# A fused attention and mixture-of-experts block: twelve uneven turns per attention unit, and one stage joined to the next

## The chip, the cores and the metric

One core of one Trainium2 chip runs the whole program in one launch. The metric is the device time of one execution in microseconds, the median of several runs. TensorE (PE) multiplies, VectorE (DVE), ScalarE (ACT) and GpSimd (POOL) work on what it leaves in PSUM, and SyncE (SP) issues most DMAs.

## The reference

Two batches of 2048 tokens of width 256, 16 heads of width 16, everything in float32:

```
mod = silu(c) @ w_mod                       # sa, ca, ga, sb, cb, gb per batch
h = layernorm(x) * (1 + ca) + sa
q = (h @ W_q + b_q) @ W_s;  k = h @ W_k + b_k;  v = h @ W_v + b_v
attn = softmax(q k^T / sqrt(16)) v          # per head, 2048 x 2048 scores
x = x + ga * (attn @ W_o + b_o)
h = layernorm(x) * (1 + cb) + sb
scores = softmax(h @ router_w + router_b)   # 8 experts
each expert takes its 512 best tokens:  relu(h1 @ w1 + b1) @ w2 + b2, times the score
x = x + gb * (sum of the experts' rows)
```

## The kernel before

The program is a row of stages, each a block in which the five engines run their own instruction lists and meet only at semaphores. All engines meet at the end of a block.

**Projection and attention** are one block already. Attention has 32 heads (2 batches of 16), each cut into two halves of 1024 queries: 64 units. A unit has three kinds of work for TensorE:

- 16 *groups* (`fill_group`, L216 to L221): two matmuls, 48 contraction rows each, 512 columns, the first on partitions 0 to 47, the second on partitions 64 to 111. They give unscaled scores with queries on partitions, only to find each query's maximum. VectorE takes the maximum of a group of 128x1024 in one instruction (`reduce_group`, L227). There are two slots of two PSUM banks, so group n may start when the reduce of group n-2 is done (`groups_out`, L904). Groups run 24 ahead of the scores.
- 32 *score chunks* (`scores`, L553 to L570): one matmul of 50 contraction rows and 512 columns. Even chunks lie on partitions 0 to 49, odd ones on 64 to 113. ScalarE takes exp of each chunk (L869) from one of three PSUM banks, so chunk n may start when the exp of chunk n-3 is done (`scores_out`).
- the *value products* (`weigh`, L908 to L926), 128 contraction rows, accumulated in bank 7. They are done in blocks: `BLOCK` = 3 chunks at a time, the first block of a unit 2 chunks, so 11 blocks and 11 turns per unit. Four column strips of 32 go side by side, in two instructions each. A block's products are issued `DELAY` = 2 turns after its scores.

One turn of TensorE (loop at L932 on) is: the value products of an old block, then three new score chunks with one or two groups among them. In five turns of a unit, which start on an even chunk, two groups stand around the scores (G0 G1 S0 S1 S0 G0 G1); in five, which start on an odd chunk, one group stands after the first score (S1 G0 G1 S0 S1); one turn has one group and two chunks (G0 G1 S0 S1). After its last product of a unit ScalarE copies the accumulator out (`take_output`, L855), between the exps of chunk 2 and 3 of the next unit.

**The post stage** is the next block (L979 to L1146). For 8 chunks of 512 tokens: output projection (`project`, L1114), residual (DVE L1047), layernorm statistics (L1053, L1058, L1061; ScalarE's square root L1022; five Newton steps L165 to L169), normalised rows (L1067), eight transposes (`turn_h2`, L1098), scale and shift (ScalarE L1010), routing logits (`route`, L1123), eight transposes back (`turn_rows`, L1132), a copy (L1017) and a store of the rows to DRAM. TensorE's order for chunk n is `turn_h2(n-2)`, `project(n)`, `route(n-2)`, `turn_rows(n-2)`; VectorE does residual, root and normalisation of chunk n in one body. The first two 2 MB pairs of expert weights are loaded at this block's start (L982, L983).

**The selection stage** is the block after it: the softmax of the logits and a search of 30 probes for each expert's threshold, in which VectorE and TensorE alternate (L1270 and L1341). Then come the expert stage's gathers and matmuls, which the change does not touch.

Of the kernel before, what the change touches and what calls it, by code (L numbers as in the profile page):

```python
# [10 lines left out]
ALU = mybir.AluOpType  # L11
# [80 lines left out]
def adaln_moe_block(nc, x, w_q, b_q, w_k, b_k, w_v, b_v, w_o, b_o, w_s, router_w, router_b,  # L92
                    w1, b1, w2, b2, c, w_mod, out):
    ctx = ExitStack()
    with ctx:
# [596 lines left out]
        xb_in, xb_ready = [sem(f"xb_in{b}") for b in range(NB)], sem("xb_ready")  # L692
        with nc.Block() as block:
            pv_done, acc_out, v_staged = sem("pv_done"), sem("acc_out"), sem("v_staged")
# [5 lines left out]
            normalised = sem("normalised")  # L700
# [3 lines left out]
            def blocks_until(n):  # L704
                u, c = divmod(n, UNIT_CHUNKS)
                return u * BLOCKS + (c - FIRST_BLOCK) // BLOCK + 2

            def chunks_of(block):
                u, b = divmod(block, BLOCKS)
                end = u * UNIT_CHUNKS + FIRST_BLOCK + b * BLOCK  # L710
                return range(end - (BLOCK if b else FIRST_BLOCK), end)
# [21 lines left out]
            def _(sp):  # L733
# [38 lines left out]
                for u in range(UNITS):  # L772
# [15 lines left out]
                    if u % HALVES and u // HALVES + NBUF < G:  # L788
                        load_next(u // HALVES)
                finish_group(UNITS - 2)  # L790
                store_output(UNITS - 1)
                load_output(UNITS - 1)

            @block.gpsimd
            def _(pool):
# [38 lines left out]
                for u in range(1, UNITS):  # L834
# [10 lines left out]
                    if u > 2 and done % HG == HG - 1:  # L845
                        normalise_part(done // HG, f)

            @block.scalar
            def _(act):
# [7 lines left out]
                for n in range(STEPS * 2):  # L857
                    if n % UNIT_CHUNKS == BLOCK and n > UNIT_CHUNKS:
                        take_output(n // UNIT_CHUNKS - 1)
# [11 lines left out]
                take_output(UNITS - 1)  # L871

            @block.vector
            def _(dve):
# [13 lines left out]
                invert(UNITS - 2)  # L888

            @block.tensor  # L890
            def _(pe):
# [41 lines left out]
                for block in range(DELAY, blocks):  # L933
                    weigh(block - DELAY)
                    b = block % BLOCKS
                    many = FIRST_BLOCK if b == DELAY else BLOCK
                    twice = b != DELAY and (b == 0 or b > DELAY and b % 2 == 1) or block == 2 * DELAY
                    for n in range(many):
                        if n == (0 if twice or b == DELAY else 1) and group < STEPS:
                            next_group(group)  # L940
                            group += 1
                        scores(pe, *divmod(chunk, 2))
                        chunk += 1
                    if twice and group < STEPS:
# [6 lines left out]
        h2_t = pt[:, 1:4:2, :].rearrange("p s (k t) -> p s k t", k=KD)  # L951
        ao_c = stage_a[:].rearrange("p s (t d) -> p s t d", d=D)
        xn2 = stage_b[:].rearrange("p s (t d) -> p s t d", d=D)
        h2_c = pt[:, 0:4:2, :].rearrange("p s (t d) -> p s t d", d=D)
        w_slots = v_all[:].rearrange("p t d -> p (t d)").rearrange("p (s n) -> p s n", s=2)
        w1_sb = [w_slots[:, s, 0:KD * FF].rearrange("p (k f) -> p k f", k=KD) for s in range(2)]
        w2_sb = [w_slots[:, s, KD * FF:].rearrange("p (f d) -> p f d", f=NF) for s in range(2)]
        w1_v = w1.rearrange("e (k p) f -> e p k f", p=P)
        w2_v = w2.rearrange("e (f p) d -> e p f d", p=P)
        w1_h = [kp[:, s, :].rearrange("p (k f) -> p k f", k=KD) for s in range(2)]  # L960
        weights_in = [sem(f"weights_in{s}") for s in range(2)]
        w1_high, w1_low = sem("w1_high"), sem("w1_low")

        def take_w1_high(act, e):
            act.wait_ge(weights_in[e % 2], e // 2 * 32 + 32)
            nc.scalar.copy(w1_h[e % 2], w1_sb[e % 2]).then_inc(w1_high, 1)

        out_stored = sem("out_stored")
        h2_stored = [sem(f"h2_stored{p}") for p in range(2)]
        h2_ready, xn2_ready, rows_turned = (sem(n) for n in ("h2_ready", "xn2_ready", "rows_turned"))  # L970
        y_full, y_out = sem("y_full"), sem("y_out")
        h2_turned, h2t_ready, l_full, l_out = sem("h2_turned"), sem("h2t_ready"), sem("l_full"), sem("l_out")
        var2_done, root2_done = sem("var2_done"), sem("root2_done")
        b_of = lambda n: slice(n // NCH, n // NCH + 1)

        with nc.Block() as block:
            @block.sync
            def _(sp):
                for par in range(2):  # L979
                    sp.sem_inc(h2_stored[par], 16)  # L980
                for e in range(2):
                    sp.dma_start(w1_sb[e], w1_v[e]).then_inc(weights_in[e], 16)  # L982
                    sp.dma_start(w2_sb[e], w2_v[e]).then_inc(weights_in[e], 16)  # L983
                for n in range(chunks):
                    if n == 2:
                        sp.wait_ge(normalised, G // HG * HALVES - 2)
                        load_inverse(sp, G // HG - 1, 1)
                    rows = slice(n * CT, (n + 1) * CT)
                    sp.wait_ge(y_out, n * 2 + 4)
                    sp.dma_start(out_rows[:, rows, :], xb[:, rows, :]).then_inc(out_stored, 16)  # L990
                    sp.wait_ge(h2_ready, n * 2 + 2)
                    sp.dma_start(h2_rows[:, rows, :], h2_c[:, n % 2]).then_inc(h2_stored[n % 2], 16)
                sp.wait_ge(out_stored, 16 * chunks)
                for par in range(2):
                    sp.wait_ge(h2_stored[par], 16 * pairs + 16)

            @block.gpsimd
            def _(pool):
                for f in range(HALVES):
                    pool.wait_ge(o_in[f], G * 32)  # L1000
                    pool.wait_ge(inverse_in[f], G * 16)
                    normalise(nc.gpsimd, G // HG - 1, f).then_inc(normalised, 1)

            @block.scalar
            def _(act):
                def take_h2(n, par):
                    act.wait_ge(h2_turned, n + 3)
                    act.wait_ge(l_full, n + 1)
                    for k in range(KD):
                        nc.scalar.activation(h2_t[:, par, k, :], bank(4 + k), ACT.Identity,  # L1010
                                             bias=mod_col[:, 2, k, b_of(n)], scale=mod_col[:, 3, k, b_of(n)]).then_inc(h2t_ready, 1)

                def take_rows(n, par):
                    act.wait_ge(rows_turned, n + 1)
                    act.wait_ge(h2_stored[par], n // 2 * 16 + 16)
                    for half in range(2):
                        nc.scalar.copy(h2_c[:, par, 2 * half:2 * half + 2, :],  # L1017
                                       bank(half).rearrange("p (t d) -> p t d", d=D)).then_inc(h2_ready, 1)

                def root(n, par):  # L1020
                    act.wait_ge(var2_done, n + 1)
                    nc.scalar.activation(nwt[:, 1, par * CT:(par + 1) * CT], nwt[:, 0, par * CT:(par + 1) * CT],  # L1022
                                         ACT.Sqrt).then_inc(root2_done, 1)

                act.sem_inc(h2t_ready, 2)
                for n in range(chunks):
                    if n > 1:
                        take_h2(n - 2, n % 2)
                    root(n, n % 2)
                    if n > 1:  # L1030
                        take_rows(n - 2, n % 2)
                for n in range(chunks - 2, chunks):
                    take_h2(n, n % 2)
                    take_rows(n, n % 2)

            @block.vector
            def _(dve):
                link, v = links["dve"], nc.vector
                dve.sem_inc(l_out, 2)
                dve.sem_inc(y_out, 2)  # L1040

                def body(n, par, logits_of):
                    for half in range(2):

                        dve.wait_ge(y_full, n * 2 + (half + 5))
                        rows = xb[:, bass.ds(n * CT + half * 2, 2), :]
                        v.tensor_tensor(rows, bank(2 + half).rearrange("p (t d) -> p t d", d=D), rows,  # L1047
                                        ALU.add).then_inc(y_out, 1)
# [583 lines left out]
```

## Time and profile before

| | us |
|---|---|
| median of 3 runs (lowest, highest) | 1806.25 (1805.63, 1806.42) |
| the profiled execution | 1805.18 |
| its span, first to last instruction | 1803.2 |
| attention, from the first value product to the last | 143 to 1406 |
| post stage | 1412 to 1486 |
| selection stage | 1486 to about 1570 |

The span is some 2 us under its execution's time, and that execution is 1.1 us under the median. The stage borders are read from the timeline. In a timeline the start of a matmul can be trusted more than its end, which is modelled, so durations of a turn are taken from start to start.

### The profile page before, as it was taken

To read this page: it belongs to the slowest core of one execution; us is meant where nothing else is said; L and a number is where in the kernel's file an instruction comes from. 1 tells how busy PE (TensorE), PEld (TensorE's weight loads), DVE (VectorE), ACT (ScalarE), POOL (GpSimd) and SP (SyncE) were. 2 spreads that over 40 slices of the span, in tenths; PEclk is the share of its full clock that TensorE was granted. 3 is DMA by queue.
4 is the path that set the end of the run, shared out by engine and by line. 5 is a ranking of instruction groups with operands and counts; after the bars stand their busy time and mean duration, and the time that the engine had idled before them with its cause. 6 is when DMAs were issued, how large, how long until landed. Compare 5 with 4: busy or idle time off the path is not lost. (4 is left out here: it accounts for less than half of the span.)

```text
span 1803.2 us, 42958 instructions
## 1 busy us (share of the span) xinstructions
PE 1692.5 (94%) x16862; PEld 951.5 (53%) x16862; DVE 1495.3 (83%) x1964; ACT 1215.3 (67%) x2304; POOL 245.8 (14%) x306
## 2 busy tenths in 40 slices
PE   7999999999999999999999999999999771599997
PEld 4645555555555555555555555555554670267886
DVE  5579999999999999999999999999995458645652
ACT  2327888888888888888888888888888330022231
POOL 0332013000000000000000000000000001235553
PEclk9999999999999999999999999999999885599999
DMA  7560442222233222223322222332200440025342
GB/s 253 189 180 28 101 97 39 38 41 38 52 64 52 38 40 40 38 52 63 51 41 39 41 37 52 61 53 41 39 14 14 145 164 0 24 74 137 83 128 24
DMA packets 93652, 121.95 MB, mean 68 GB/s; under 512 B 24060, under 2 KB 70716, under 8 KB 90348
## 3 DMA queue, kind: packets, MB, share of 16 engines
q1 hardware_dynamic: 84492, 109.22, 26.9%
q0 software_dynamic: 6144, 8.39, 2.7%
q8 instruction: 133, 2.18, 0.5%
q10 hardware_dynamic: 2816, 1.61, 0.3%
q14 instruction: 67, 0.55, 0.1%
HBM read 79.35 MB, written 38.54 MB: 65 GB/s over the span
## 5 line engine op out<-in xcount | busy, mean ns | idle before, releaser
L227 DVE TENSOR_REDUCE pmax<-ps 128x2 f32<-128x1024 f32 x1024 | 1192.6, 1216 | 53.2 <-PE ps L220 46.3
L869 ACT ACTIVATE pt<-ps 128x512 f32<-128x512 f32 x2048 | 1077.7, 599 | 181.4 <-PE ps L569 170.3
L220 PE MATMUL ps<-kp,qp 48*128 48x512 f32 x2048 | 626.5, 464 | 2.4 <-DVE pmax L227 2.4
L923 PE MATMUL ps<-pt,v_st 128*32 128x256 f32 (+1 forms) x10752 | 589.7, 335 | 0.2 <-ACT pt L869 0.2
L569 PE MATMUL ps<-qp,kp 50*128 50x512 f32 x2048 | 562.5, 422 | 0.5 <-ACT pt L869 0.5
L569 PEld LDWEIGHTS ps<-qp,kp 50*128 50x128 f32 x2048 | 294.4, 185 | 258.7 <-ACT pt L869 250.9
L923 PEld LDWEIGHTS ps<-pt,v_st 128*32 128x32 f32 x10752 | 265.7, 109 | 265.3 <-issue 192.3
L220 PEld LDWEIGHTS ps<-kp,qp 48*128 48x128 f32 x2048 | 246.1, 184 | 115.0 <-issue 90.0
L1452 ACT ACTIVATE ao<-ps,b_col 128x512 f32<-128x512 f32 x64 | 44.0, 688 | 156.5 <-PE ps L1591 156.5
L210 POOL CAST m_parts<-rowmax_t 128x32 fp32r<-128x32 f32 x64 | 13.4, 210 | 839.7 <-DVE rowmax_t L239 839.7
L1605 PE MATMUL ps<-v_all,ao 128*128 128x256 f32 x512 | 112.5, 381 | 0.8 <-ACT ao L1452 0.8
L1605 PEld LDWEIGHTS ps<-v_all,ao 128*128 128x128 f32 x512 | 96.7, 190 | 14.1 <-ACT ao L1452 1.2
L431 ACT ACTIVATE pt<-ps,xb 128x512 fp32r<-128x512 f32 x32 | 22.0, 687 | 61.3 <-PE ps L594 61.3
L1527 DVE TENSOR_TENSOR pt<-ps,b_row 128x256 f32<-128x256 f32 x32 | 13.5, 422 | 57.9 <-PE ps L1605 57.9
L594 PE MATMUL ps<-pt,xb 128*128 128x512 f32 x128 | 59.1, 603 | 1.7 <-ACT pt L415 1.7
L1420 POOL DMA_INDIRECT y<-pt,scatter_at x32 | 54.8, 1711 | 33.3 <-DVE pt L1531 24.9
L798 POOL COPY v_st<-v_all 128x256 f32<-128x256 f32 x32 | 12.6, 397 | 293.3 <-PE ps L923 293.3
L1490 DVE TENSOR_TENSOR stage_b<-lane,col_row 128x1024 bf16<-128x1024 int32 x32 | 37.7, 1222 | 13.4 <-PE ps L1564 13.1
L1444 ACT COPY list_t<-ps 128x128 f32<-128x128 f32 x8 | 2.1, 259 | 67.0 <-PE ps L1564 67.0
L1402 POOL DMA_INDIRECT stage_a<-h_rows,gather_at x32 | 33.0, 1032 | 84.5 <-DVE gather_at L1501 54.3
L1591 PE MATMUL ps<-qp,kp 128*128 128x512 f32 x96 | 40.0, 416 | 0.0
L1114 PE MATMUL ps<-wog,ao 128*128 128x256 f32 x128 | 33.3, 422 | 6.8 <-DVEq L1040 6.8
(196 smaller groups left out, 944.0 us busy)
## 6 DMA issues: line engine op xcount, KB each, us to landing
kp<-k_parts SPq DMA_DIRECT2D x186, 128.0 KB, 4.5
v_all<-L_ffn_w SPq DMA_DIRECT2D x16, 1024.0 KB, 8.4
qp<-q_parts SPq DMA_DIRECT2D x186, 64.0 KB, 4.0
q_parts<-pt SPq DMA_DIRECT2D x16, 512.0 KB, 2.7
k_parts<-pt SPq DMA_DIRECT2D x16, 512.0 KB, 3.0
o_rows<-o_sb SPq DMA_DIRECT2D x64, 128.0 KB, 2.0
sums_c<-o_rows SPq DMA_DIRECT2D x512, 0.5 KB
m_rows<-m_parts SPq DMA_DIRECT2D x256, 2.0 KB
```

What stands on the lines that cost most here:

```text
L220: last = nc.tensor.matmul(slot[:, half * CH:(half + 1) * CH], qp[rows, r, a * P:(a + 1) * P], kp[rows, r, c * CH:(c + 1) * CH], start=True ...
L227: v.reduce_max(pmax[:, u % 2, 2 * k:2 * k + 2], slot.rearrange("p (f t) -> p f t", f=2), AX.X).then_inc(groups_out, 1)
L569: nc.tensor.matmul(bank(n % SCORE_BANKS), kp[rows, h % NBUF, kt * P:(kt + 1) * P], qp[rows, h % NBUF, f * CH:(f + 1) * CH], start=True, st ...
L594: last = mm(unit_bank(n, u), w[:, k, (u % 2) * P:(u % 2 + 1) * P], h_t[n % 2][:, k, :], start=k == 0, stop=k == KD - 1)
L869: nc.scalar.activation(pt[:, s % PTS, half * CH:(half + 1) * CH], bank(n % SCORE_BANKS), ACT.Exp, scale=SCALE).then_inc(scores_out, 1)
L923: last = mm(acc[32 * j:32 * (j + 1), first * QB:(first + many) * QB], v_st[:, h % NBUF, kt, :], probs[:, :, j * QB:(j + 1) * QB], start=kt ...
L1114: last = mm(bank(2 + half)[:, t * D:(t + 1) * D], ao[:, n // NCH * KD + k, at:at + P], wog[:, n // NCH, k, :], start=k == 0, stop=k == KD - 1)
L1420: nc.gpsimd.indirect_dma_start(out_flat, bass.IndirectOffsetOnAxis(ap=scatter_at[:, par, cc:cc + 1], axis=0), contrib[:, cc, :], None, com ...
L1452: nc.scalar.activation(hid[:, f, :], bank(2 + f % 2), ACT.Relu, bias=b1_col[:, bass.ds(e * NF + f, 1)]).then_inc(hid_out, 1)
L1490: v.tensor_tensor(one_hot[:, g8 % 2], lane[:, bass.ds(n, 1), g8 * 8:(g8 + 1) * 8].squeeze(1).unsqueeze(2).broadcast_to([P, 8, P]), col_row ...
L1591: last = mm(bank(2 + f % 2), w[:, k, f * P:(f + 1) * P], t[:, k, :], start=i == 0, stop=i == len(products) - 1)
L1605: last = mm(bank(eo_banks[cc])[:, 0:D], hid[:, f, cc * P:(cc + 1) * P], w2_sb[par][:, f, :], start=f == 0, stop=f == NF - 1)
```

## The change

1. `BLOCK`, `FIRST_BLOCK` and the rule for one or two groups go. A table of twelve turns replaces them. Each entry is (chunks weighed, chunks scored, places of the groups among the scores):

```diff
-BLOCK = 3
-BLOCKS = -(-UNIT_CHUNKS // BLOCK)
-FIRST_BLOCK = UNIT_CHUNKS - (BLOCKS - 1) * BLOCK
+TURNS = ((3, 3, (1, 2)), (3, 3, (1,)), (3, 3, (1, 3)), (2, 3, (2,)), (2, 2, (1,)), (2, 2, (1,)),
+         (1, 2, (0,)), (2, 2, (1,)), (3, 3, (2, 3)), (3, 3, (2,)), (4, 3, (0, 3)), (4, 3, (1,)))
+BLOCKS = len(TURNS)
+BLOCK_ENDS = [sum(TURNS[(i + DELAY) % BLOCKS][0] for i in range(b + 1)) for b in range(BLOCKS)]
```

```diff
                 for block in range(DELAY, blocks):
                     weigh(block - DELAY)
-                    many = FIRST_BLOCK if b == DELAY else BLOCK
-                    twice = b != DELAY and (b == 0 or b > DELAY and b % 2 == 1) or block == 2 * DELAY
+                    _, many, groups_before = TURNS[block % BLOCKS]
+                    for n in range(many + 1):
+                        if n in groups_before and group < STEPS:
+                            next_group(group)
+                            group += 1
+                        if n < many:
+                            scores(pe, *divmod(chunk, 2))
+                            chunk += 1
...
+                    if block == blocks - DELAY:
+                        project_rows(pe, 0)
                 for block in range(blocks - DELAY, blocks):
                     weigh(block)
-
+                post_pe(pe)
```

2. The post stage moves into the attention block. Its instruction lists follow each engine's attention list, and chunk 0's output projection is issued before attention's last turn and last two value blocks. The orders of its engines change:

```diff
+        def post_dve(dve, link, invert_first, invert_last):
...
+            residual(0)
+            invert_first()
+            for n in range(chunks):
+                if n + 1 == 3:
+                    invert_last()
+                if n + 1 < chunks:
+                    residual(n + 1)
+                normalise_rows(n)
+                if n > 0:
+                    take_logits(n - 1)
...
+        def post_pe(pe):
...
+            project_rows(pe, 1)
+            for n in range(chunks):
+                turn_h2(n)
+                if n + 2 < chunks:
+                    project_rows(pe, n + 2)
+                route(n)
```

`residual(n)` waits for both halves of `project_rows(n)` and ends with the variance; `normalise_rows(n)` is the Newton steps and the normalised rows; `turn_h2(n)` waits for those. ScalarE takes the last unit's accumulator out after chunk 0's square root. SyncE, before attention's last unit, issues the loads of the first two experts' weights.

3. The transposes back, their copies and the row stores leave the post stage. TensorE now does them in the selection stage, half a chunk (four transposes) after every second of the 30 probe matmuls; ScalarE copies and SyncE stores there. TensorE's probe loop is unrolled:

```diff
+                    for j in range(TOPBIT + 1):
                         pe.wait_ge(counted, j + 1)
                         mm(bank(1)[:, 0:1], same[:], count[:], start=True, stop=True).then_inc(totalled, 1)
+                        if j % 2 and j // 2 + 2 < 2 * chunks:
+                            turn_rows(j // 2 + 2)
```

## Rows read from the trace of the kernel before

**Rows 1.** The page: instructions and busy share of each engine.

```profile
PE 1692.5 (94%) x16862; PEld 951.5 (53%) x16862; DVE 1495.3 (83%) x1964; ACT 1215.3 (67%) x2304; POOL 245.8 (14%) x306
```

**Rows 2.** Busy time by stage: length, engines, granted clock, DMA share, GB/s.

```profile
150.00:1375.00 1225.00, 1224.80 (x14378) 621.87 (x14379) 1175.80 (x1123) 1054.54 (x2045) 72.58 (x163) 1.00 0.27 47
1375.00:1405.00 30.00, 29.81 (x336) 14.62 (x332) 2.79 (x5) 26.47 (x53) 0.46 (x2) 1.00 0.11 30
1412.40:1486.40 74.00, 63.74 (x384) 57.78 (x384) 44.98 (x169) 21.38 (x41) 4.38 (x2) 0.87 0.51 178
1486.40:1570.00 83.60, 20.93 (x133) 10.24 (x133) 62.24 (x263) 3.00 (x6) 19.71 (x32) 0.51 0.05 13
```

**Rows 3.** Groups by line, busy, mean ns, idle before; one timeline row of VectorE.

```profile
L227 DVE TENSOR_REDUCE pmax<-ps 128x2 f32<-128x1024 f32 x1024 | 1192.6, 1216 | 53.2 <-PE ps L220 46.3
L869 ACT ACTIVATE pt<-ps 128x512 f32<-128x512 f32 x2048 | 1077.7, 599 | 181.4 <-PE ps L569 170.3
...
803.99 5.71 DVE L227 TENSOR_REDUCE pmax<-ps 128x2 f32<-128x1024 f32 x5
```

**Rows 4.** The line that copies the accumulator out, once per unit: first and last.

```profile
L855 ACT COPY o_sb<-ps x64: 372/393/395, 163.1 to 1405.7; 128x256 f32<-128x256 f32 x64
```

**Rows 5.** Timeline of TensorE in attention: start, length, line, operands, count.

```profile
801.83 0.50 PE L220 MATMUL ps<-kp,qp 48*128 48x512 f32 x2
...
802.98 0.86 PE L923 MATMUL ps<-pt,v_st 128*32 128x128 f32 x16
...
807.58 0.49 PE L569 MATMUL ps<-qp,kp 50*128 50x512 f32 x1
...
808.48 0.86 PE L923 MATMUL ps<-pt,v_st 128*32 128x256 f32 x16
...
815.87 0.64 PE L923 MATMUL ps<-pt,v_st 128*32 128x256 f32 x8
816.44 0.50 PE L220 MATMUL ps<-kp,qp 48*128 48x512 f32 x2
816.78 0.40 PE L569 MATMUL ps<-qp,kp 50*128 50x512 f32 x2
817.11 0.86 PE L923 MATMUL ps<-pt,v_st 128*32 128x256 f32 x16
817.89 0.50 PE L220 MATMUL ps<-kp,qp 48*128 48x512 f32 x2
```

**Rows 6.** Timeline of TensorE: the end of a turn with two groups.

```profile
809.84 0.46 PE L220 MATMUL ps<-kp,qp 48*128 48x512 f32 x1
809.85 0.45 PE L569 MATMUL ps<-qp,kp 50*128 50x512 f32 x1
...
810.13 0.39 PE L220 MATMUL ps<-kp,qp 48*128 48x512 f32 x1
```

**Rows 7.** Timeline between attention's last value block and the selection stage's first instruction.

```profile
1404.78 0.86 PE L923 MATMUL ps<-pt,v_st 128*32 128x128 f32 x16 [0.19 <-ACT pt L869]
...
1412.48 10.19 PE L1114 MATMUL ps<-wog,ao 128*128 128x256 f32 x32 [6.84 <-DVEq L1040]
...
1486.47 0.25 DVE L1251 TENSOR_SCALAR same_i<-iota_i 128x128 int32<-128x128 int32 x1 [6.00 <-PEq L976]
```

**Rows 8.** Timeline of one chunk of the post stage, VectorE and TensorE.

```profile
1451.92 0.69 DVE L1047 TENSOR_TENSOR xb<-ps,xb 128x512 f32<-128x512 f32 x1 [0.72 <-PE ps L1114]
...
1454.33 1.04 PE L1098 MATMUL ps<-ident,stage_b 128*128 128x128 f32 x8
...
1455.15 0.18 DVE L165 RECIPROCAL rstd<-nwt 128x4 f32<-128x4 f32 x1 [0.27 <-ACT nwt L1022]
1455.20 3.62 PE L1114 MATMUL ps<-wog,ao 128*128 128x256 f32 x16
...
1456.15 1.39 DVE L1067 TENSOR_SCALAR stage_b<-xb,mv,rstd 128x256 f32<-128x256 f32 x4
```

**Rows 9.** Timeline of TensorE at the post stage's end, after it had stood idle.

```profile
1471.36 1.95 PE L1123 MATMUL ps<-rw_sb,pt 128*128 128x8 f32 x16 [2.11 <-ACT pt L1010]
...
1474.83 1.91 PE L1098 MATMUL ps<-ident,stage_b 128*128 128x128 f32 x8
```

More of the change, by code:

```diff
@@ new lines, in y_bank, with turned_bank, logits_bank, post_sp @@
+        def y_bank(half):
+            return bank(3 + half)
+        def turned_bank(k):
+            return bank(5 + k)
+        def logits_bank(n):
+            return bank(2 + 5 * (n % 2))
+        b_of = lambda n: slice(n // NCH, n // NCH + 1)
+        def post_sp(sp, load_last_inverse):
+            for n in range(chunks):
+                if n == 2:
+                    load_last_inverse()
+                rows = slice(n * CT, (n + 1) * CT)
+                sp.wait_ge(y_out, n * 2 + 2)
+                sp.dma_start(out_rows[:, rows, :], xb[:, rows, :]).then_inc(out_stored, 16)
+            sp.wait_ge(out_stored, 16 * chunks)
@@ new lines, in project_rows @@
+        def project_rows(pe, n):
+            if n == 0:
+                pe.wait_ge(xb_ready, 2 * NB)
+                pe.wait_ge(groups_out, STEPS)
+                pe.wait_ge(normalised, G // HG // NB * HALVES)
+            if n >= NCH and n % 2 == 0:
+                pe.wait_ge(normalised, (G // HG - 1) * HALVES + (n - NCH) // 2 + 1)
+            for half in range(2):
+                if n > 0:
+                    pe.wait_ge(y_out, n * 2 + half - 1)
+                for t in range(2):
+                    at = (n % NCH) * CH + (half * 2 + t) * P
+                    for k in range(KD):
+                        last = nc.tensor.matmul(y_bank(half)[:, t * D:(t + 1) * D], ao[:, n // NCH * KD + k, at:at + P],
+                                                wog[:, n // NCH, k, :], start=k == 0, stop=k == KD - 1)
+                last.then_inc(y_full, 1)
@@ new lines, in post_pe, with turn_h2, route @@
+        def post_pe(pe):
+            def turn_h2(n):
+                pe.wait_ge(xn2_ready, n + 1)
+                if n > 0:
+                    pe.wait_ge(h2t_ready, n * 2)
+                for k in range(KD):
+                    for t in range(CT):
+                        last = nc.tensor.transpose(turned_bank(k)[:, t * P:(t + 1) * P], xn2[:, n % 2, t, k * P:(k + 1) * P], ident[:])
+                last.then_inc(h2_turned, 1)
+            def route(n):
+                pe.wait_ge(h2t_ready, n * 2 + 2)
+                if n == 1:
+                    pe.wait_ge(acc_out, UNITS)
+                if n > 1:
+                    pe.wait_ge(l_out, n - 1)
+                for t in range(CT):
+                    for k in range(KD):
+                        last = nc.tensor.matmul(logits_bank(n)[:, t * E:(t + 1) * E], h2_of(n)[:, k, t * P:(t + 1) * P],
+                                                rw_sb[:, k, :], start=k == 0, stop=k == KD - 1)
+                last.then_inc(l_full, 1)
+            project_rows(pe, 1)
+            for n in range(chunks):
+                turn_h2(n)
+                if n + 2 < chunks:
+                    project_rows(pe, n + 2)
+                route(n)
@@ L846, in _ @@
                         normalise_part(done // HG, f)
+                for f in range(HALVES):
+                    normalise_part(G // HG - 1, f)
             @block.scalar
@@ L940, in _ @@
                             next_group(group)
                             group += 1
-                        scores(pe, *divmod(chunk, 2))
-                        chunk += 1
-                    if twice and group < STEPS:
+                        if n < many:
+                            scores(pe, *divmod(chunk, 2))
+                            chunk += 1
+                    if block == 2 * DELAY:
                         next_group(group)
                         group += 1
+                    if block == blocks - DELAY:
+                        project_rows(pe, 0)
@@ L1206, in adaln_moe_block, with _ @@
             with nc.Block() as block:
+                @block.sync
+                def _(sp):
+                    for n in range(chunks):
+                        sp.wait_ge(h2_ready, n * 2 + 2)
+                        sp.dma_start(h2_rows[:, n * CT:(n + 1) * CT, :], h2_c[:, n % 2]).then_inc(h2_stored[n % 2], 16)
+                    for par in range(2):
+                        sp.wait_ge(h2_stored[par], 16 * pairs)
                 @block.gpsimd
@@ L1245, in _ @@
                     nc.scalar.activation(logits[:], logits[:], ACT.Exp).then_inc(exps_done, 1)
+                    for g in range(2 * chunks):
+                        n, half = divmod(g, 2)
+                        act.wait_ge(rows_turned, g + 1)
+                        if n > 1 and half == 0:
+                            act.wait_ge(h2_stored[n % 2], n // 2 * 16)
+                        nc.scalar.copy(h2_c[:, n % 2, half * 2:half * 2 + 2, :],
+                                       bank(6 + half).rearrange("p (t d) -> p t d", d=D)).then_inc(h2_ready, 1)
                 @block.vector
```

294 lines of the change are left out of this document (107 added, 187 removed).

## The prediction

> **What bounds the kernel now.** I read the page first [rows 1]. TensorE is busy 94% of the span and VectorE 83%. A busy TensorE in this profile may be waiting inside an instruction, so I then read the busy times by stage [rows 2]. The stretch from 150 to 1375 us holds two thirds of the time; in it TensorE is booked full at the full clock, VectorE 96%, ScalarE 86%. Which of the three sets the pace?
>
> The accumulator is copied out once per unit, so the first and last copy give the unit's length: (1405.7 - 163.1) / 63 = 19.72 us [rows 4]. VectorE needs for its 16 reduces one start every (5.71 - 1.22) / 4 = 1.12 us when it never waits [rows 3], 17.9 us a unit, and some 0.5 us for the two small steps at a unit's end: 18.5. ScalarE's exps were busy 1077.7 / 64 = 16.8 us a unit [rows 3]. So both have over a microsecond to spare, and VectorE's idle time before its reduces, 53.2 us in all [rows 3], is time in which TensorE was late. TensorE is the bound, and what counts is what one turn of it costs.
>
> The timeline gives that, start to start [rows 5]. A turn has a value part and a score part.
>
> - Value part: 2 chunks take 816.44 - 815.87 = 0.57 us, 3 chunks 817.89 - 817.11 = 0.78. So 0.21 a chunk and 0.15 per turn.
> - Score part: the two matmuls of a group stand in one row of 0.50 us, x2, as long as one alone (0.49, x1); so do an even and an odd score (0.40, x2). They lie on different halves of the partitions and run side by side. I call such a pair, or one matmul left alone, a *slot*. G0G1 | S0S1 is 2 slots: 817.11 - 816.44 = 0.67 us. S1G0 | G1S0 | S1 is 3 slots: 808.48 - 807.58 = 0.90. G0G1 | S0S1 | S0 | G0G1 is 4: 802.98 - 801.83 = 1.15. Some 0.23 to 0.25 per slot and 0.2 per turn.
>
> Only neighbours in the program pair. [Rows 6] show it: the group's first matmul is booked beside a score on the same partitions, at 809.84, and its partner starts only at 810.13, 0.29 us later. It did not slip ahead beside the lone score.
>
> Counted so, the present unit needs: value parts 11 x 0.15 + 32 x 0.21 = 8.37; score parts 5 x 1.15 + 5 x 0.90 + 0.67 = 10.92; together 19.29. The other 0.43 us of the 19.72 are waits, for exps (three banks) and reduces (two slots).
>
> **The change, part 1: twelve turns.** What can be won is the 0.43 us of waits. What is added comes out of the table. One more turn: 0.15 us in the value part and the 0.2 fixed in the score part. And the order of scores and groups changes which matmuls are neighbours. From turn 2, with the parity of the chunk:
>
> - turns 2, 8, 10, 0 have two groups and come to 4 slots each (turn 2: S0 | G0G1 | S1S0 | G0G1; turn 0: S0 | G0G1 | S1G0 | G1S0)
> - turns 3, 9, 11, 1 have one group and 3 scores or 3 slots each (S1S0 | G0G1 | S1 or S1G0 | G1S0 | S1)
> - turns 4, 5, 7 have one group between two scores: S0 | G0G1 | S1. Four matmuls in 3 slots, where G0G1 | S0S1 would have been 2
> - turn 6 is G0G1 | S0S1, 2 slots
>
> So 4 x 1.15 + 7 x 0.90 + 0.67 = 11.57, value parts 12 x 0.15 + 6.72 = 8.52, together 20.09 us, against 19.72 measured now. I followed the events through one unit with the starts above (a reduce every 1.12 us, an exp every 0.53, which is 1077.7 / 2048 in [rows 3]): with twelve smaller turns hardly a wait is left, so I take 20.09 as it stands. That is +0.37 us a unit. Some 61 units run with all three kinds of work: +22.6 us. From both sides: if the waits stay at half, +0.58 a unit, +35 us. On the other side five turns (0, 2, 4, 5, 7) now begin with a lone score right behind the value products. No row shows that. In the present kernel the first slot behind them takes 816.78 - 816.44 = 0.34 instead of 0.23; if a lone first score hides in that, 5 x 0.11 = 0.55 us come off, and the unit is 19.54 plus waits: -11 us or less. I take the upper figure, since the pair there takes 0.50 us for both, no longer than one alone [rows 5], so the extra time is not the second one's.
>
> A rule speaks further against the new order. The Trainium skill, "TensorE: Matmul & The Clock Gate", section "Part 3: Packing small matmuls", says matmuls start and end strictly in program order and that a weight load overlaps running matmuls only when its row group differs. By it each lone score that is followed by a group on its own rows would also pay for the load; [rows 6] show 0.06 of that (0.29 for 0.23), and three such places (turns 4, 5, 7) are not in my 0.90. It would make 0.2 us a unit more, +11 us, by an estimate from these rows.
>
> The end of attention, 1.6 units without groups (second row of [rows 2]), waits for exps and changes little: 0, within 1 us.
>
> **Part 2: the joined post stage.** Won: the gap from the last value block, 1404.78 + 0.86, to the first projection at 1412.48, 6.8 us [rows 7], and transposes back (8 of about 0.12 us) from a TensorE-bound stage. Chunk 0's projection, 3.6 us [rows 8], now lies before the last turn; behind it the exps catch up, which hides about 0.8, so attention ends 2.8 us later, at 1408.4 on the old clock. Projection 1 follows at once and ends at 1412.1.
>
> What is late next is the new order. VectorE does `residual(n+1)` before `normalise_rows(n)`, and TensorE does `project_rows(n+2)` after `turn_h2(n)`, which waits for `normalise_rows(n)`. So VectorE, done with chunk n's rows, waits for a projection that starts only now; nothing overlaps but `route`. One lap, from rows ready to rows ready: 0.06 wake-up; transposes 1455.20 - 1454.33 = 0.87; projection 3.62 + 0.04; from the second half's residual to normalised rows 1456.15 - 1451.92 = 4.23 less 0.27 waited for the root = 3.96; rows 1.39 [rows 8]. Sum 9.9 us, at the full clock. The present loop overlaps all this and takes about 7 us a chunk (8 in the 74 us of [rows 2], third row). In a lap TensorE works 0.87 + 3.6 + 1.9 (the routing, 1.95 in [rows 9]) and then stands about 3.5 us. After standing 2.11 us in the present kernel its eight transposes took 1.91 instead of 1.04 [rows 8, 9], and after 6.84 us the 32 projection matmuls took 10.19, so 5.1 per chunk instead of 3.62 [rows 7]: the clock is then at its lower level, 1.2 GHz (0.87 granted over the stage, [rows 2]). With 1.9 and 5.1 the lap is 12.3 us. Part of each lap will run at 2.4 GHz; I take 11.5. The Trainium skill's same page, section "HAM oscillation", describes such a loop, cold again after every gap; it would give the 12.3.
>
> Rows of chunk 0 are ready at 1412.1 + 3.96 + 1.39 = 1417.5; six laps, 69 us; then the last two chunks' transposes, scale and routing, about 11 us (one chunk with rows back and store took 1486.47 - 1474.83 = 11.6 [rows 7, 9]; two without these take about as long). The selection stage starts at 1497.5 instead of 1486.5: +11 us, between 0 (9.9 a lap) and +17 (12.3).
>
> The last unit's accumulator, stores, inverses and the POOL product have until the third lap (chunk 4) and the fifth (chunk 6): 1437 and 1457; they need some 12 and 30 us from 1409, so they are hidden, and would cost a few us if not. SyncE's four weight loads wait behind a staging that is long done, and DMA is 11 to 27% busy there [rows 2]: 0.
>
> **Part 3: transposes in the selection.** TensorE is busy 20.9 of 83.6 us there (fourth row of [rows 2]). Four cold transposes take 0.95 us (half of 1.91, [rows 9]) between two probe matmuls. VectorE needs about 1 us to come with its next count, so they are just hidden: +1, between 0 and +13 (14 times 0.95).
>
> **The sum.** Span 1803.2 + 22.6 + 11 + 1 = 1837.8; the profiled execution lay 2.0 above its span, and the median 1.1 above that: 1841. I say 1840.
>
> **Rivals.**
> 1. *The lone first score hides behind the switch from value products*, and waits of about 0.1 are left: 19.64 us a unit, -5 us; with the post stage +11 and +1: 1813. Against it, the 0.50 us of the first pair. 0.15.
> 2. *The unit gains, and the whole is faster.* The array lets S0, G0, G1, S1 finish in two slots (the odd half running ahead), and the lone score hides. Turns 4, 5, 7 cost 0.67: 3 x 0.23 + 0.55 = 1.24 off 20.09, 18.85, so VectorE's 18.5 and waits set it: about 19.2, 0.5 less than now, -31 us; with +12 behind it 1787. It decides from a unit of 19.5. Against it [rows 6]; for it, that nothing shows the matmul behind such a pair. With only half of that gain 1797 to 1803. 0.22 in all.
> 3. *The clock stays at 2.4 GHz in the post stage*: laps of 9.9, 1840 - 11 = 1829. 0.15, since 2.11 us of standing was enough once.
> 4. *The twelve turns do nothing* (waits come back as fast as turns shrink): +0, post +12: 1818. 0.08.
> My forecast, 1840, has 0.40; its own range is 1827 to 1853.
>
> A measurement here can tell 0.2%, 3.6 us, from no change. Faster: rival 2, 0.22. Within: the lucky edge of rivals 1 and 2, 0.08. Slower: the rest, 0.70. The range, to hold it 8 times in 10, goes from 1798, inside rival 2, to 1851.
>
> **What the profile after would show.** The accumulator copies 20.1 us apart (19.5 or less would refute the slots). VectorE's idle before its reduces risen, from 53 to about 75 us, and ScalarE's too. A turn S0 G0 G1 S1 of 0.90 from first start to next value block, not 0.67. In the post stage normalised rows 10 to 12 us apart, VectorE waiting for the projection about 4 us in each, clock rows between 0.5 and 1. Half-chunk transposes between probes, with the probes' spacing unchanged. Rows of the post stage 7 us apart would make part 2 wrong.

## The result, and the profile after

The changed kernel takes 1830.2 us in the median of 4 runs (1829.2 to 1831.1), against 1806.3 for the kernel before on the same chip: a ratio of 1.0136, 95% interval 1.0120 to 1.0152. It is slower. I had forecast 1840, with 1798 to 1851 as the range.

First the rows of the new page that answer to [rows 1] and [rows 3]. Then the stages that answer to [rows 2], with the columns as there: attention, the post stage, the selection stage.

```profile
PE 1712.4 (94%) x17374; PEld 994.0 (54%) x17374; DVE 1495.9 (82%) x1964; ACT 1221.5 (67%) x2304; POOL 245.6 (13%) x306
...
L229 DVE TENSOR_REDUCE pmax<-ps 128x2 f32<-128x1024 f32 x1024 | 1188.5, 1216 | 62.9 <-PE ps L222 55.0
L1046 ACT ACTIVATE pt<-ps 128x512 f32<-128x512 f32 x2048 | 1076.4, 598 | 186.7 <-PE ps L571 166.6
```

```profile
150.00:1375.00 1225.00, 1220.30 (x14794) 648.65 (x14796) 1166.26 (x1118) 1052.86 (x2035) 72.47 (x163) 1.00 0.27 47
...
1414.00:1512.70 98.70, 65.16 (x304) 58.11 (x305) 45.87 (x158) 13.87 (x27) 4.72 (x3) 0.74 0.17 56
1512.70:1596.00 83.30, 36.62 (x199) 21.10 (x200) 62.75 (x264) 12.74 (x22) 19.59 (x32) 0.51 0.19 64
```

Busy totals hardly tell the two kernels apart. The stages do. The post stage, from the last value block to the first selection instruction, now takes 98.7 us; before it took 1486.47 - 1405.64 = 80.8 [rows 7], although a gap of 6.8 us was taken out of it. Its granted clock is 0.74, where it was 0.87 behind that gap [rows 2].

The unit is read from the accumulator's copies, as in [rows 4]:

```profile
L1032 ACT COPY o_sb<-ps x64: 353/374/394, 162.1 to 1414.5; 128x256 f32<-128x256 f32 x64
```

(1414.5 - 162.1) / 63 = 19.88 us instead of 19.72. The last of these 63 intervals has chunk 0's projection in it; the mean of the 61 before the last two is 19.86, against 19.77.

The 25.5 us between the two spans are: attention ends 8.4 us later; the post stage is 17.9 longer; selection and experts are 0.8 shorter. Attention's start moves by more than a microsecond between the runs of this case (141.9 to 145.0 us), and I did not look for the reason. From the first copy of the accumulator to the end of the last value block, which leaves the start out, the changed kernel takes 1251.9 us and the kernel before 1242.6.

One lap of the new post stage, VectorE and TensorE, answers to [rows 8]:

```profile
1460.36 1.38 DVE L789 TENSOR_SCALAR stage_b<-xb,mv,rstd 128x256 f32<-128x256 f32 x4
...
1461.79 1.97 PE L837 MATMUL ps<-ident,stage_b 128*128 128x128 f32 x8 [3.45 <-DVE stage_b L789]
1463.56 5.66 PE L826 MATMUL ps<-wog,ao 128*128 128x256 f32 x16
...
1467.21 0.69 DVE L770 TENSOR_TENSOR xb<-ps,xb 128x512 f32<-128x512 f32 x1 [5.38 <-PE ps L826]
1469.05 1.85 PE L848 MATMUL ps<-rw_sb,ao 128*128 128x8 f32 x16
1469.25 0.69 DVE L770 TENSOR_TENSOR xb<-ps,xb 128x512 f32<-128x512 f32 x1 [1.34 <-PE ps L826]
...
1472.91 1.38 DVE L789 TENSOR_SCALAR stage_b<-xb,mv,rstd 128x256 f32<-128x256 f32 x4
```

Two waits feed each other here. TensorE stands 3.45 us for VectorE's rows; then its transposes (1.97 us, at the lower clock; 1.04 at the full one [rows 8]) and its projection come one after another while VectorE stands 5.38 us. From rows to rows it is 12.55 us.

### The profile page after: what moved, and what is told of

Same layout as the page of the kernel before. It is cut to its first block and busy times, and to the rows that moved or that the text cites. A ratio compares the mean times of both kernels' runs of the same rounds, so it can differ in the third digit from the quotient of the medians.

```text
span 1828.7 us, 43907 instructions
## 1 busy us (share of the span) xinstructions
PE 1712.4 (94%) x17374; PEld 994.0 (54%) x17374; DVE 1495.9 (82%) x1964; ACT 1221.5 (67%) x2304; POOL 245.6 (13%) x306
## 5 line engine op out<-in xcount | busy, mean ns | idle before, releaser
L229 DVE TENSOR_REDUCE pmax<-ps 128x2 f32<-128x1024 f32 x1024 | 1188.5, 1216 | 62.9 <-PE ps L222 55.0
L571 PE MATMUL ps<-qp,kp 50*128 50x512 f32 x2048 | 644.3, 439 | 0.5 <-ACT pt L1046 0.5
L1105 PE MATMUL ps<-pt,v_st 128*32 128x128 f32 (+1 forms) x11264 | 603.3, 328 | 0.7 <-ACT pt L1046 0.7
L222 PE MATMUL ps<-kp,qp 48*128 48x512 f32 x2048 | 581.8, 443 | 7.3 <-DVE pmax L229 2.5
L1105 PEld LDWEIGHTS ps<-pt,v_st 128*32 128x32 f32 x11264 | 274.1, 109 | 301.3 <-issue 134.0
L571 PEld LDWEIGHTS ps<-qp,kp 50*128 50x128 f32 x2048 | 303.3, 185 | 215.8 <-ACT pt L1046 145.4
L222 PEld LDWEIGHTS ps<-kp,qp 48*128 48x128 f32 x2048 | 241.7, 184 | 98.5 <-DVE pmax L229 50.4
L212 POOL CAST m_parts<-rowmax_t 128x32 fp32r<-128x32 f32 x64 | 13.4, 210 | 838.0 <-DVE rowmax_t L241 838.0
L770 DVE TENSOR_TENSOR xb<-ps,xb 128x512 f32<-128x512 f32 x16 | 11.1, 692 | 66.8 <-PE ps L826 66.8
L1541 DVE TENSOR_TENSOR pt<-ps,b_row 128x256 f32<-128x256 f32 x32 | 13.5, 422 | 58.2 <-PE ps L1619 58.2
L837 PE MATMUL ps<-ident,stage_b 128*128 128x128 f32 x64 | 15.6, 424 | 29.9 <-DVE stage_b L789 29.9
```

What stands on the lines that cost most here:

```text
L222: last = nc.tensor.matmul(slot[:, half * CH:(half + 1) * CH], qp[rows, r, a * P:(a + 1) * P], kp[rows, r, c * CH:(c + 1) * CH], start=True ...
L229: v.reduce_max(pmax[:, u % 2, 2 * k:2 * k + 2], slot.rearrange("p (f t) -> p f t", f=2), AX.X).then_inc(groups_out, 1)
L571: nc.tensor.matmul(bank(n % SCORE_BANKS), kp[rows, h % NBUF, kt * P:(kt + 1) * P], qp[rows, h % NBUF, f * CH:(f + 1) * CH], start=True, st ...
L1105: last = mm(acc[32 * j:32 * (j + 1), first * QB:(first + many) * QB], v_st[:, h % NBUF, kt, :], probs[:, :, j * QB:(j + 1) * QB], start=kt ...
```

## The experiments

Each kernel was run beside the kernel before on the same chip. Where a unit is given for a kernel with the joined stage, it is (last copy - first copy) / 63, which holds 0.04 to 0.05 us of chunk 0's projection; compare it with 19.88.

**The twelve turns alone.** The kernel before with part 1 of the change (the diff of part 1 without its `project_rows` line).

> The kernel before with the table of twelve turns and nothing else of the change. Theory A (the turns cost little: in the changed kernel the accumulator copies lay 19.88 us apart against 19.72): 62 units at +0.1 to +0.16 us, so 1806.3 + 8 = 1814, unit 19.86, post stage as before. Rival B (my count of slots, 20.09 us a unit): +22.6, 1829. Rival C (the turns are free or better and all of the loss is the joined stage): 1806 or less.

Measured: 1811.7 us, ratio 1.0035 (1.0021 to 1.0049).

```profile
L856 ACT COPY o_sb<-ps x64: 366/375/393, 163.2 to 1411.4; 128x256 f32<-128x256 f32 x64
```

(1411.4 - 163.2) / 63 = 19.81 us, 0.09 above the kernel before. So the table costs 6.7 us, and my 0.37 us a unit was four times too much.

**The joined stage alone.** The changed kernel with the old turns written as a table.

```diff
-TURNS = ((3, 3, (1, 2)), (3, 3, (1,)), (3, 3, (1, 3)), (2, 3, (2,)), (2, 2, (1,)), (2, 2, (1,)),
-         (1, 2, (0,)), (2, 2, (1,)), (3, 3, (2, 3)), (3, 3, (2,)), (4, 3, (0, 3)), (4, 3, (1,)))
+TURNS = ((3, 3, (0, 3)), (3, 3, (1,)), (2, 2, (0,)), (3, 3, (0, 3)), (3, 3, (1,)), (3, 3, (0, 3)),
+         (3, 3, (1,)), (3, 3, (0, 3)), (3, 3, (1,)), (3, 3, (0, 3)), (3, 3, (1,)))
```

> The changed kernel with the eleven turns of the kernel before put back (as a table: one or two groups and 3, 3, 2, 3 ... chunks as they stood). Theory A (the two parts add up): the twelve turns alone cost 6 to 7 us, so the joined stage alone gives 1805 + 25 - 6.5 = 1823.5, the unit falls from 19.86 to 19.76 us, the post stage keeps its laps of 12. Rival B (the parts interact, the twelve turns are needed by the joined tail or hurt it): more than 3 us away from that.

Measured: 1825.0 us, ratio 1.0104 (1.0088 to 1.0121). 1.0104 x 1.0035 is 1.0139, the whole change's 1.0136: the parts add up. The joined stage is three quarters of the loss. Its attention, from the first copy to the end of the last value block, takes 1246.1 us against 1242.6 before, with units as long as before (19.77 us in the mean of the same 61). So chunk 0's projection costs 3.5 us there.

**How the array pairs matmuls.** In the changed kernel turns 4, 5 and 7 are S0 G0 G1 S1. Here is one, the third line the next value block:

```profile
802.44 0.49 PE L571 MATMUL ps<-qp,kp 50*128 50x512 f32 x1
802.45 0.72 PE L222 MATMUL ps<-kp,qp 48*128 48x512 f32 x2
...
803.11 0.65 PE L1105 MATMUL ps<-pt,v_st 128*32 128x128 f32 x16
```

803.11 - 802.44 = 0.67 us, the time of two slots, where I had counted three. It is the median of all 183 such turns.

The timeline merges the group's two matmuls into one row, but the trace behind it holds them apart, since only the second one, G1, raises the semaphore that VectorE waits for. There S0 starts at 802.444, G1 at 802.451, G0 at 802.777 and S1 at 802.789: G1, on the upper half, starts beside S0, a third of a microsecond ahead of G0, which stands before it in the program. G1 starts ahead of G0 in all 183.

The test adds matmuls on one half of the partitions only. `low_again` is 2 in turns 4, 5 and 7:

```diff
-            for half in range(2):
+            for half in [0] * low_again + [0, 1]:
                 rows = slice(HALF * half, HALF * half + KROWS)
                 last = nc.tensor.matmul(slot[:, half * CH:(half + 1) * CH], qp[rows, r, a * P:(a + 1) * P],
...
```

> The changed kernel; in turns 4, 5 and 7 (two chunks) the group's first matmul, on the lower half of the partitions, is issued three times, which writes the same values again. The order there is S0 G0 G0 G0 G1 S1. The score part of these turns takes 0.67 us in the changed kernel. Theory A (each half of the partitions is a lane of its own; a lane runs its matmuls one after another and does not wait for the order of the other): lower lane 4, upper lane 2, so 4 slots, 1.13 us. Rival B (any two run side by side): 6 / 2 = 3 slots, 0.90. Rival C (only neighbours on different halves pair, as I predicted): S0, G0, G0, G0G1, S1, 5 slots, 1.36. By A the unit grows by about 3 x 0.45 less the wait of turn 8, so by 1.0 to 1.3 us, and the time by 60 to 80.

Measured, one run: 1895.1 us, unit 20.9. One such turn, and the start of the next:

```profile
816.30 0.50 PE L571 MATMUL ps<-qp,kp 50*128 50x512 f32 x1
816.32 0.72 PE L222 MATMUL ps<-kp,qp 48*128 48x512 f32 x2
816.65 0.40 PE L571 MATMUL ps<-qp,kp 50*128 50x512 f32 x1
816.88 0.62 PE L222 MATMUL ps<-kp,qp 48*128 48x512 f32 x2
817.43 0.64 PE L1105 MATMUL ps<-pt,v_st 128*32 128x128 f32 x16
818.00 0.50 PE L571 MATMUL ps<-qp,kp 50*128 50x512 f32 x1
```

817.43 - 816.30 = 1.13 us: four slots, and 1.13 is the median of these turns too. There are six matmuls, four of them on the lower half. If any two could pair it would be 0.90, if only neighbours, 1.36. The single records show the same: on the upper half G1 starts at 816.32 and S1 at 816.65; on the lower half S0 at 816.30 and the three of the group at 816.64, 816.88 and 817.11. So each half of the partitions is a lane with its own order, and a turn's score part lasts as long as its fuller lane.

**The order that I thought cheaper.** The group ahead of both scores in those turns.

```diff
-(2, 2, (1,)), (2, 2, (1,)), (1, 2, (0,)), (2, 2, (1,))
+(2, 2, (0,)), (2, 2, (0,)), (1, 2, (0,)), (2, 2, (0,))
```

> The changed kernel with the group ahead of both scores in turns 4, 5 and 7: G0 G1 S0 S1 instead of S0 G0 G1 S1. My prediction counted 2 slots for this order and 3 for the present one. Rival C of the lane run (only neighbours pair): 3 x 0.23 us a unit less, 19.2 us, 1829 - 43 = 1786. Theory A (two lanes, each of two matmuls in either order): the turns stay at 0.67 us, the unit at 19.86 within 0.05, 1826 to 1833.

Measured: 1829.4 us, ratio 1.0135 (1.0118 to 1.0151). Nothing moved. The turn G0 G1 S0 S1 takes 0.67 us here, as S0 G0 G1 S1 did: there are two matmuls per lane in either order.

**The wait that is left.** By lanes the new table has 4 turns of four slots, 4 of three and 4 of two: 4 x 1.15 + 4 x 0.90 + 4 x 0.67 = 10.88, with the value parts' 8.52 a unit of 19.40. Measured 19.86, so 0.46 us of waits. Most of it is in turn 8:

```profile
806.08 5.71 DVE L229 TENSOR_REDUCE pmax<-ps 128x2 f32<-128x1024 f32 x5
...
806.62 0.86 PE L1105 MATMUL ps<-pt,v_st 128*32 128x256 f32 x16
807.40 0.50 PE L571 MATMUL ps<-qp,kp 50*128 50x512 f32 x2
807.74 0.39 PE L222 MATMUL ps<-kp,qp 48*128 48x512 f32 x2
807.97 0.39 PE L571 MATMUL ps<-qp,kp 50*128 50x512 f32 x1
808.44 0.50 PE L222 MATMUL ps<-kp,qp 48*128 48x512 f32 x2
808.87 0.86 PE L1105 MATMUL ps<-pt,v_st 128*32 128x128 f32 x16
```

From the score at 807.97 to the group at 808.44 it is 0.47 us instead of 0.23. The first row says why. The second of its five reduces runs from 807.18 to 808.39 in the trace, and it is the one that frees the group's PSUM slot. The group behind this standstill takes 0.43 us to the next value block. The score part is 808.87 - 807.40 = 1.47, not 1.15. The test moves one group a turn later:

```diff
-(3, 3, (2, 3)), (3, 3, (2,)), (4, 3, (0, 3)), (4, 3, (1,))
+(3, 3, (2,)), (3, 3, (0, 3)), (4, 3, (0, 3)), (4, 3, (1,))
```

> The changed kernel with one group moved from turn 8 to turn 9: turn 8 (3, 3, (2,)), turn 9 (3, 3, (0, 3)). In turn 8 the last group stands 0.47 us in the lane before it starts, the largest wait of the unit: it waits for the reduce of the group two before it. Theory A (that wait is lost time of the lane): turn 8 falls from 2.26 to about 1.67 us, turn 9 rises from 1.69 to 1.92 to 1.95, so the unit is 0.2 to 0.35 us shorter, 19.5 to 19.65: 12 to 21 us off 1829, 1808 to 1817. Rival B (VectorE or the exps are the bound and the wait only moves to another turn): unit 19.8 or more, 1825 to 1830.

Measured: 1816.7 us, ratio 1.0058 (1.0042 to 1.0075), 13.5 us less than the whole change.

```profile
L1032 ACT COPY o_sb<-ps x64: 353/376/394, 162.7 to 1401.8; 128x256 f32<-128x256 f32 x64
```

(1401.8 - 162.7) / 63 = 19.67 us instead of 19.88. The wait was real, and no other engine took its place. In the mean of the 61 intervals a unit now takes 19.65 us, less than the 19.77 of the old eleven turns.

**Is it the clock?** Six matmuls that nobody reads, after the routing of chunks 0 to 5, keep TensorE at work in the lap's gap.

```diff
                 route(n)
+                if n + 2 < chunks:
+                    for _ in range(6):
+                        nc.tensor.matmul(bank(0)[:, 0:D], ident[:], wog[:, 0, 0, :], start=True, stop=True)
```

> The changed kernel with six matmuls of 128x256 that nobody reads, after each routing of the post stage, into a bank that is free: 2.5 us of work at the full clock where TensorE now stands 3.5 us a lap. Theory A (laps of 12 us are 9.9 us of serial work plus the lower clock): the clock stays at 2.4 GHz, laps of 10.0 to 10.5, six laps give back 9 to 12 us: 1820. Rival B (the clock does not matter to the lap): laps of 12 or more and 1830 to 1836.

Measured: 1818.9 us, ratio 1.0075 (1.0060 to 1.0091), 11 us less than the change, although there is more work in it.

```profile
1460.30 1.09 PE L837 MATMUL ps<-ident,stage_b 128*128 128x128 f32 x8 [0.76 <-DVE stage_b L789]
1461.23 3.62 PE L826 MATMUL ps<-wog,ao 128*128 128x256 f32 x16
1464.68 1.85 PE L848 MATMUL ps<-rw_sb,ao 128*128 128x8 f32 x16
1466.39 2.84 PE L860 MATMUL ps<-wog,ident 128*128 128x256 f32 x12
1469.98 1.09 PE L837 MATMUL ps<-ident,stage_b 128*128 128x128 f32 x8 [0.76 <-DVE stage_b L789]
```

The lap is 1469.98 - 1460.30 = 9.68 us at the full clock. Four of the six laps were 9.7 us. The other two, 11.4 and 13.4, ran partly at the lower clock (0.84 and 0.85 granted), and in the longer one VectorE stood for a product of POOL (it multiplies the attention output by the inverses of the sums; the last section tells of it). In the changed kernel the six laps took 12.2 us in the mean, and 12.0 without the one that has such a product in it. So a lap there is 9.7 us of serial work and about 2.3 of clock.

**Which swap opens the loop.** Two kernels, each the changed one with two lines of a list exchanged. First TensorE's:

```diff
             for n in range(chunks):
-                turn_h2(n)
                 if n + 2 < chunks:
                     project_rows(pe, n + 2)
+                turn_h2(n)
                 route(n)
```

> The changed kernel with one swap in TensorE's post list: project_rows(n + 2) before turn_h2(n). Theory A (the serial lap of rows, transposes, projection, residual is what costs): residual(n+2) no longer waits for the transposes; TensorE's lap becomes projection 3.3, transposes 0.9, a wait of 1.6 for ScalarE, routing 1.9, together 7.7 us at the full clock instead of 12 us now; six laps and the tail give back about 27 us: 1803. Rival B (the laps are long because of something else, the clock alone or ScalarE): laps stay above 11 us and the time within 6 us of 1830.

Measured: 1811.5 us, ratio 1.0039 (1.0024 to 1.0054), 18.7 us less than the change where I had expected 27. The six laps were 5.5, 14.0, 7.5, 7.9, 9.6 and 9.6 us. In the one of 14.0 the routing and the projection ran at the lower clock and VectorE stood for a product of POOL.

```profile
1457.33 1.95 PE L848 MATMUL ps<-rw_sb,ao 128*128 128x8 f32 x16 [1.54 <-ACT ao L746]
...
1459.13 5.39 PE L826 MATMUL ps<-wog,ao 128*128 128x256 f32 x16
```

Routing now follows right behind the transposes and waits for ScalarE's scale and shift; the next projection stands behind it. The wait was exchanged for another one, of 1.54 us in every lap, and in some laps the clock fell behind it (5.39 us for this projection, 3.62 at the full clock).

Then VectorE's:

```diff
             for n in range(chunks):
                 if n + 1 == 3:
                     invert_last()
+                normalise_rows(n)
                 if n + 1 < chunks:
                     residual(n + 1)
-                normalise_rows(n)
```

> The changed kernel with one swap in VectorE's post list: normalise_rows(n) before residual(n + 1). TensorE's list stays. Theory A (the serial lap): VectorE then has a projection done ahead, and TensorE works transposes 0.9, projection 3.3, routing 1.9 without a wait, so laps of 6.1 to 6.9 us at the full clock; seven laps of 6.6 instead of 75.7 us in all, and the first rows some 5 us earlier: 32 to 38 us less, 1791 to 1797, under the kernel before. Rival B (the swap of the lists is not it; projection stays behind the wait, as with TensorE's swap, which left laps of 7.5 to 9.6): laps of 8 or more, 1805 or more.

Measured: 1791.2 us, ratio 0.9919 (0.9903 to 0.9936): 39 us less than the change, and faster than the kernel before.

```profile
1446.22 1.07 PE L837 MATMUL ps<-ident,stage_b 128*128 128x128 f32 x8
1447.13 3.62 PE L826 MATMUL ps<-wog,ao 128*128 128x256 f32 x16
1450.59 1.85 PE L848 MATMUL ps<-rw_sb,ao 128*128 128x8 f32 x16
1452.29 1.07 PE L837 MATMUL ps<-ident,stage_b 128*128 128x128 f32 x8
```

TensorE goes from transposes to projection to routing without standing, 6.07 us a lap here. VectorE's rows come 5.92 to 6.06 us apart, but for two laps of 7.7 and 7.9 with POOL's products in them. The post stage takes 58.1 us (1414.8 to 1472.9) instead of 98.7.

**Both parts mended.** The same swap with the old turns, and with the new table after its group was moved.

> Eleven turns as before, the joined stage, and VectorE's normalise_rows(n) before residual(n + 1). If both parts' costs are what the runs before say and add up, 1794 less 6.5 for the turns: 1785 to 1791, 0.8 to 1.1% under the kernel before. If the twelve turns help the tail: above 1791.

Measured: 1784.5 us, ratio 0.9881 (0.9865 to 0.9898). With VectorE's lines in this order the joined stage alone saves 20.5 us, where it cost 20.0.

> Twelve turns with one group moved from turn 8 to turn 9, and VectorE's rows before the next residual. If both gains add up (12.5 us for the group, 38 us for the order of lists): 1791 less 12.5, 1776 to 1782, under the eleven turns with the same order (1784.5), so that the twelve turns pay once their one long wait is gone. If the unit's gain is lost again beside the faster tail: 1784 or more.

Measured: 1777.5 us, ratio 0.9848 (0.9832 to 0.9865), beside a kernel before of 1804.2 us. It is the fastest version here. The twelve turns with the moved group beat the old eleven by 0.0033 of the time, about 6 us. The two intervals just touch, and the two kernels ran on different chips; the unit, 19.64 us against 19.77 in the two traces, says the same and gives about 8 us.

## Why the prediction was right, and where its terms were off

The direction held, and both parts of the change cost time, as forecast. The size was 10 us too large, and that it was not further off is luck. I gave 22.6 us to the twelve turns and 12 to the joined stage; alone they cost 6.7 and 20.0. The two errors half cancelled.

1. *A unit is bound by TensorE's turns, and the table adds to them.* Right in kind, wrong in size: 0.37 us a unit forecast, 0.09 measured with the turns alone. Two terms of that sum failed. The slot count: "turns 4, 5, 7 ... four matmuls in 3 slots" at 0.90 each; they took 0.67, which is 0.69 us a unit too much. I had read it out of [rows 6], and read them wrongly. I took the record at 809.84 for the group's first matmul. In the trace it is the one that raises the group's semaphore, so it is the second, on the upper half, and it starts beside the lone score on the lower half; the record at 810.13 is the first. So the group's second matmul did slip ahead, as it does in 253 of the 304 full turns with two groups of the kernel before. The length of such a turn could not have told me, since its lower lane has four matmuls and gives four slots under both readings; the single records could. And the waits: "hardly a wait is left", where 0.46 us were left. My hand count had turn 8's second group just in time; the reduce that it needed was still running. The old unit had 0.43 by the same sum. So by lanes the change takes one slot away, adds one turn, and leaves the waits as large as they were.
2. *The lone first score.* There was nothing to hide or to add. A turn that starts with a lone score and one that starts with a pair both take 0.67 us when each lane has two matmuls.
3. *The rule on the weight loads.* The Trainium skill, "TensorE: Matmul & The Clock Gate", section "Part 3: Packing small matmuls", says that a weight load overlaps only matmuls of another row group, by which these turns would cost 0.2 us a unit more. It is not borne out: 0.67 us is the time of G0 G1 S0 S1 too, both in the same kernel and in the run with the group first. Nor does that section's strict program order of starts fit: G1 starts 0.33 us ahead of G0 in the turns above.
4. *Rival 2* had the right mechanism, the odd half running ahead, and the wrong end. It took 0.55 us more off for the lone score and left 0.35 for waits, which made 19.2. Nothing came off for the lone score, and the waits were 0.46.
5. *Chunk 0's projection* inside attention: 2.8 us forecast, 3.5 measured.
6. *The serial lap*: 9.9 at the full clock forecast, 9.7 measured with the filler. This step was right, and the swap of VectorE's two lines shows it: 39 us. With the clock I took 11.5; the six laps took 73.3 us, 12.2 each, 4.3 us more. Of these 4.3 a product of POOL made about 1.9, and the clock the rest. The Trainium skill, "TensorE: Matmul & The Clock Gate", section "HAM oscillation", describes a loop that is cold again after every gap; the transposes behind the gap took 1.87 to 1.97 us in every lap, which agrees. The 12.3 us that I had worked out for such a lap was the better guess. Two bounds were also summed too wide: laps of 9.9 and 12.3 us put the post stage's part at 1.4 and 15.8 us, where I wrote 0 and 17.
7. *Before and after the laps*: from attention's end to chunk 0's rows 9.1 us forecast, 10.9 measured. The end, from chunk 6's rows, 11 forecast, 14.5 measured: two routings at the lower clock, 3.58 us each instead of 1.85.

```profile
1501.66 3.58 PE L848 MATMUL ps<-rw_sb,ao 128*128 128x8 f32 x16 [1.54 <-ACT ao L746]
...
1508.59 3.58 PE L848 MATMUL ps<-rw_sb,ao 128*128 128x8 f32 x16 [1.54 <-ACT ao L746]
```

   I had costed that end by the kernel before's last chunk alone.
8. *Transposes in the selection*: 1 us forecast within 0 to 13; the stage did not get longer. They fit between two probes:

```profile
1526.37 0.18 PE L1356 MATMUL ps<-count,same 128*128 128x1 bf16 x1 [1.09 <-DVE above L1272]
1526.41 1.09 PE L1343 MATMUL ps<-ident,ao 128*128 128x128 f32 x4
1527.65 0.18 PE L1356 MATMUL ps<-count,same 128*128 128x1 bf16 x1
```

   The probes are 1.28 us apart, as before, with the transposes between them.
9. *The inverses, stores and POOL products are hidden*: nearly. No projection of the changed kernel waited for them, but their product held VectorE up (below).

Attention came out about 17 us better than forecast, the post stage 10 us worse, the selection 2 us better. The other signs that I had named: VectorE's idle time before its reduces rose to 62.9 us, not 75, and in a lap it waited 5.4 us for the projection, not 4.

What stays open: the 0.2 us of waits that remain in the unit after the group was moved (19.65 against about 19.4 by slots), and whether a better table exists. Only one group was moved.

## What to carry to other kernels

When two engines hand work to and fro in a software pipeline, count how many items lie between them in both lists together: putting VectorE's finish one item later took away just the slack that TensorE's list had, and the loop went serial, although each list alone looked pipelined. Exchanging two lines was worth 39 us here, and decided whether the join of the stages saved 20.5 us or cost 20.0. And before a cost rule for a new instruction order is read from a trace, make sure which instruction each record is, for instance by the semaphore that it raises. The trace of the kernel before held the answer, and I had two records the wrong way round.

## What the runs showed of the hardware

**Two row lanes.** Matmuls of 48 and 50 contraction rows on the two halves of the partitions ran as two queues. S0 G0 G1 S1 and G0 G1 S0 S1 take 0.67 us alike; two more on one half make it 1.13. So balance the halves within a turn; between these two orders it made no difference.

**Starts leave the program's order, completions are told in it.** In the turn shown G1's record ends at 802.95 and G0's at 803.17. The semaphore that G1 raises rises at 803.20, not before G0 is done. The changed kernel's trace has 440 groups whose second matmul started 0.1 us or more ahead of the first. In their median the semaphore rises 0.02 us behind the end of the first one and 0.25 behind the end of the second. So the semaphore on a group's last matmul still covers the whole group.

**A wait costs more than itself.** The first slot behind value products takes 0.34 us instead of 0.23 [rows 5]. A pair behind a standstill also takes 0.1 us more: 808.44 to 808.87 above is 0.43, where a last pair without one takes 817.11 - 816.78 = 0.33 [rows 5].

**POOL's product stops some VectorE instructions.** While POOL multiplied 128x1024 floats in SBUF, a VectorE instruction of four elements took 2.34 us instead of 0.17:

```profile
1420.24 2.34 POOL L894 TENSOR_TENSOR ao<-ao,stage_a 128x1024 f32<-128x1024 f32 x1 [37.30 <-DMA stage_a<-inverse_sums]
1420.27 2.34 DVE L779 TENSOR_SCALAR nwt<-mv 128x4 f32<-128x4 f32 x1
```

In the run with rows first both products did this: in the first lap a Newton step took 1.70 us instead of 0.16, in the fourth the row instruction 3.41 instead of 1.38, in laps of 7.7 and 7.9 us among laps of 5.9 to 6.1. The Trainium skill, "SBUF — State Buffer", section "Terms", says that GpSimd and VectorE share one pair of ports, which is locked for a whole instruction, while the loser fully blocks; these rows agree, down to the end of the stopped instruction, 0.03 us behind the product's. The 2.2 us lost above more than cover the 1.8 us of point 7's first half. The kernel before had both products too and lost nothing: the first ran while VectorE stood idle, the second beside a residual that VectorE reads from PSUM, 0.69 us as elsewhere.
